# The opening of a fused transformer kernel put in another order: x and queries loaded first, the mask behind them; keys, values and score maxima dealt out in single blocks

## The chip, the cores and the metric

The kernel runs on one core of a Trainium2 chip. The metric is device time in microseconds (us) of one execution; the median of three runs is what is compared. The engines are TensorE (PE in the profile; its weight loads are PEld), VectorE (DVE), ScalarE (ACT), GpSimd (POOL) and SyncE (SP), which here only issues transfers.

## What is computed

Two layers on a batch of 2 with 256 rows of 256 channels, and a context of 4096 rows. Only the first attention matters for this change:

```python
h = layernorm(x)                                   # (2, 256, 256)
q = h @ Wq.T + bq ; k = ctx @ Wk.T + bk ; v = ctx @ Wv.T + bv      # 16 heads of 16
energy = where(mask == 0, -1e9, q @ k.T / sqrt(16))                # (2, 16, 256, 4096)
x = x + (softmax(energy) @ v) @ Wo.T + bo
```

Behind it come a gated convolution block, a quantised feed-forward block, a second cross-attention with an additive mask, a self-attention with rotary positions and a routed feed-forward block. They are the same in both kernels.

## The kernel before, in words

Every engine has its own program, written out by hand in `build`; the order in each is that of the code, and semaphores tie them together. All tiles lie in one SBUF tensor, `arena`, and one PSUM tensor, `psum`, so the trace names only these two; line numbers tell the steps apart.

**Keys, values, units.** The context of batch 0 is taken in 8 chunks of 512 rows. `project_keys(0, c, f)` (L1728) multiplies chunk `c` with half `f` of the key weights: one 128x512 block in float32, which the trace shows as 4 matmul records. `project_values(0, c, i)` (L1738) makes half a chunk of values, 8 records of 128x256. Both write into a ring of three PSUM banks (4 to 6), which ScalarE empties: `copy_keys` (L725, L726: a bf16 copy and a float32 copy) and `copy_values` (L731). Scores must be as exact as float32, so each key piece is split into three bf16 parts: VectorE takes the rest and casts it (`split_keys`, L1084, L1086), GpSimd makes the third part (`low_part`, L647), SyncE stores the parts in DRAM (`store_k`, L461) and loads them again stacked by head, 6 rows of parts to each channel (`load_stack`, L469: 6 transfers for a quarter of the context, two chunks). Queries take the same way (`split_queries`, L1069 to L1076; `store_queries`, L489; `load_queries`, L497). The pieces go through three float32 buffers `K32` and six places `KPT`, in the order of `piece_number`.

**Maxima.** Softmax needs each row's maximum. A *unit* is `scores(n)` (L1756): two 96x512 matmuls in bf16 into one of two pairs of PSUM banks; `row_tops(n)` (L1100) on VectorE reduces the 128x1024 result to a column of maxima. Unit n waits for the maximum of unit n - 2 (semaphore `s_maxed`). There are 32 units for the first head group; units 0 to 7 need quarter 0 of the stack, 8 to 15 quarter 1, and so on. Only when all 32 are done can `turn_max` (L1770) and the first turned scores (L1785) run, from which on exponentials (L748) and weighted values (L1803) take their turn.

**The opening.** PE first does key blocks, the transposes of the normalised x (`turn_x`, L1861) and the query projections (`project_queries_of`, L1869), with key blocks between. VectorE turns the mask into bf16 in 8 parts (`mask_part`, L1093), PE sums them (L1895), VectorE reads the sum (L1192, L1194) and writes a flag: PE branches on it (L2114) into a version without mask matmuls, `attend(False)`. The inputs have no masked place, so this version runs.

**Rounds.** In `attend` rounds `c` from 4 to 10 follow. In each half of a round PE does one key block (while c < 8), one value block of four matmuls, and then the 2 or 3 units that `UNITS_AT` gives it, in one run. VectorE does the split of the key piece and then the maxima.

**Loads.** SyncE issues the key weights, the columns of biases, x, the query and value weights, and chunks 3 to 5; ScalarE issues chunks 0 to 2 and the mask (4 transfers of 1 MB) at once. There are six slots for chunks; 6 and 7 follow when the values of chunks 0 and 1 are copied.

## Time and profile before

| | us |
|---|---|
| median of 3 runs (lowest to highest) | 1007.73 (1007.71 to 1008.43) |
| the profiled execution's own time | 1003.05 |
| its span in the trace | 1001.0 |
| PE busy | 905.0 (90%) |
| VectorE busy | 604.5 (60%) |
| ScalarE busy | 479.5 (48%) |
| first turned scores start (L1785) | 120.03 |

The span runs from the first to the last instruction of the profiled execution; the execution's own time is 2.05 us longer. All times of instructions below are counted from the span's start. A row of the timeline gives start, duration, engine, line and tiles, how many instructions it merges, and in brackets how long the engine had been idle and what ended that. PEclk is the granted TensorE clock, 1.00 being 2.4 GHz and 0.50 being 1.2 GHz.

### The profile page before, as it was taken

The page shows a single profiled execution, that of the slowest core. Times are in us where ns is not written, and L with a number is a line of the kernel's source. Part 1 is how long each engine was busy: PE and PEld are TensorE (multiplying, and loading weights), DVE is VectorE, ACT ScalarE, POOL GpSimd, SP SyncE. Part 2 cuts the span into 40 slices and gives each one's busy share as a digit, 9 for nine tenths or more (in the row PEclk, how much of TensorE's full clock was granted, in tenths as well). Part 3 has the DMA queues.
Part 4 walks back from the last instruction along what each step waited for, and adds up shares of the span by engine and source line. Part 5 has one row for each costly group of instructions (what it writes and reads, how often), then busy time and mean ns, then how long its engine had stood idle before and what let it go on. Part 6 is the DMA issues. An engine that isn't in the chain of part 4 may idle for free.

```text
span 1001.0 us, 15431 instructions
## 1 busy us (share of the span) xinstructions
PE 905.0 (90%) x6066; PEld 540.6 (54%) x6068; DVE 604.5 (60%) x1075; ACT 479.5 (48%) x951; POOL 105.7 (11%) x118
## 2 busy tenths in 40 slices
PE   6786799999999999999998899588999989988788
PEld 3444444444555555455544677354875854555656
DVE  3876577787885447888843586858414127188240
ACT  2232366777775557777788532225213110676111
POOL 1421011111000000000000200101000007155000
PEclk9999899999999999999999999779999989999889
DMA  9772823445323112222522700705438350000000
GB/s 358 218 202 93 259 79 107 133 127 163 101 66 105 33 32 65 64 67 74 191 96 76 261 1 1 253 25 184 163 133 303 118 168 1 1 1 2 0 1 22
DMA packets 68837, 108.70 MB, mean 109 GB/s; under 512 B 7062, under 2 KB 42902, under 8 KB 66838
## 3 DMA queue, kind: packets, MB, share of 16 engines
q1 hardware_dynamic: 67372, 101.92, 32.0%
q10 hardware_dynamic: 1392, 5.77, 1.4%
...
## 4 chain that ended last, share of the span: by engine, by line
PE 79%; DVE 8%; ACT 7%; issue 3%; DMA 2%; SPq 0%; POOL 0%; ACTq 0%; DVEq 0%
PE psum L1803 13%; PE psum L1785 11%; PE psum L1756 10%; PE psum L2172 6%; PE psum L2145 5%; PE psum L1934 5%; PE psum L1738 5%; PE psum L1728 4%; PE psum L2265 4%; PE psum L1947 3%; ACT arena L748 3%; DVE arena L1100 2%; PE psum L2313 2%; PE psum L2401 1%; PE psum L2298 1%
## 5 line engine op out<-in xcount | busy, mean ns | idle before, releaser
L1100 DVE TENSOR_REDUCE arena<-psum 128x1 f32<-128x1024 f32 x256 | 300.5, 1218 | 111.6 <-PE psum L1756 111.5
L748 ACT ACTIVATE arena<-psum 128x512 f32<-128x512 f32 x512 | 264.7, 604 | 63.4 <-PE psum L1785 62.3
L1785 PE MATMUL psum<-arena 99*128 99x256 bf16 x1024 | 161.0, 275 | 10.4 <-ACT arena L748 4.8
L1756 PE MATMUL psum<-arena 96*128 96x512 bf16 x512 | 152.2, 383 | 18.1 <-DVE arena L1100 11.4
L1785 PEld LDWEIGHTS psum<-arena 99*128 99x128 bf16 x1024 | 80.0, 97 | 109.2 <-ACT arena L748 50.6
L1803 PE MATMUL psum<-arena 128*32 128x256 f32 x2048 | 136.8, 385 | 0.0
L1803 PEld LDWEIGHTS psum<-arena 128*32 128x32 f32 x2048 | 53.5, 109 | 75.5 <-ACT arena L748 36.9
L1728 PE MATMUL psum<-arena 128*128 128x512 f32 x128 | 64.2, 630 | 5.6 <-DMA arena<-ctxT 5.6
L1756 PEld LDWEIGHTS psum<-arena 96*128 96x128 bf16 x512 | 49.3, 99 | 35.7 <-DVE arena L1100 18.8
L1738 PE MATMUL psum<-arena 128*128 128x256 f32 x256 | 64.2, 395 | 1.0 <-ACT arena L726 1.0
L647 POOL TENSOR_TENSOR arena<-arena 128x512 bf16<-128x512 f32 x34 | 41.5, 1221 | 210.0 <-DVE arena L1086 202.3
L2172 PE MATMUL psum<-arena 128*128 128x256 f32 x256 | 59.9, 389 | 0.0
L1738 PEld LDWEIGHTS psum<-arena 128*128 128x128 f32 x256 | 48.6, 196 | 19.6 <-issue 13.4
L2145 PE MATMUL psum<-arena 128*128 128x512 f32 x128 | 56.1, 593 | 0.0
L725 ACT ACTIVATE arena<-psum,arena 128x512 bf16<-128x512 f32 x32 | 22.0, 687 | 66.5 <-PE psum L1728 49.8
L731 ACT ACTIVATE arena<-psum 128x512 f32<-128x512 f32 x32 | 19.1, 597 | 71.1 <-PE psum L1738 71.1
L2172 PEld LDWEIGHTS psum<-arena 128*128 128x128 f32 x256 | 49.1, 196 | 6.5
L1934 PE MATMUL psum<-arena 128*128 128x256 f32 x192 | 47.0, 404 | 3.5 <-ACT arena L812 0.9
L1934 PEld LDWEIGHTS psum<-arena 128*128 128x128 f32 x192 | 38.2, 202 | 11.1 <-ACT arena L920 1.3
L2265 PE MATMUL psum<-arena 128*128 128x512 f32 x96 | 43.2, 611 | 0.7 <-ACT arena L810 0.7
L1728 PEld LDWEIGHTS psum<-arena 128*128 128x128 f32 x128 | 24.5, 200 | 29.3 <-issue 22.1
L1947 PE MATMUL psum<-arena 128*128 128x256 f32 (+1 forms) x160 | 36.4, 388 | 4.2 <-ACT arena L908 2.2
...
## 6 DMA issues: line engine op xcount, KB each, us to landing
...
kparts<-arena SPq DMA_DIRECT2D x32, 384.0 KB, 3.3
...
arena<-mask ACTq DMA_DIRECT2D x4, 1024.0 KB, 13.4
...
```

The costliest lines, as they stand in the source:

```text
L748: nc.scalar.activation(PR[step % 4][:, pair * CH:(pair + 1) * CH], ring_bank(slot), ACT.Exp)\
L1100: nc.vector.tensor_reduce(MX[g % 2][:, col:col + 1], unit_banks(n).rearrange("p b n -> p (b n)"), AX.X, ALU.max).then_inc(s_maxed, 1)
L1728: last = nc.tensor.matmul(ring_bank(slot), WK[:, k, f * P:(f + 1) * P], CTX[n % SLOTS][:, k, :], start=(k == 0), stop=(k == CT - 1))
L1738: last = nc.tensor.matmul(ring_bank(slot)[:, v * 256:(v + 1) * 256], CTX[n % SLOTS][:, k, (2 * i + v) * P:(2 * i + v + 1) * P], WV[:, k, : ...
L1756: last = nc.tensor.matmul(out, q, KST[g % 2][0:ROWS, j, at], start=True, stop=not masked, skip_group_check=True)
L1785: last = nc.tensor.matmul(ring_heads(slot)[:, u, :], KST[gg % 2][0:KROWS, j, kc * P:(kc + 1) * P], QST[0:KROWS, G * g + j, b * S:(b + 1) * S],
L1803: last = nc.tensor.matmul(PV[32 * j:32 * (j + 1), :], V_flat[:, at:at + 32], PR[step % 4][:, j * S:(j + 1) * S], start=(kc == 0), stop=(kc ...
L1934: last = nc.tensor.matmul(out, weights[:, k, m * P:m * P + width], xs[k], start=(k == 0), stop=(k == n - 1))
L1947: last = nc.tensor.matmul(out, lhs[k], weights[:, k, :], start=(k == 0 and not biased), stop=(k == n - 1), skip_group_check=biased)
L2145: last = nc.tensor.matmul(psum[:, unit % 3, :], QC[:, c, w * P:(w + 1) * P], CTXT[w // 2][:, c, n * 512:(n + 1) * 512], start=(c == 0), st ...
L2172: last = nc.tensor.matmul(psum[:, 6, 0:256], PT1[:, k * P:(k + 1) * P], CTXK[w // 2][:, k, :], start=(k == 0), stop=(k == KC - 1), skip_gr ...
L2265: last = nc.tensor.matmul(psum[:, bank, :], HTF[:, c, i * P:(i + 1) * P], WQKV[which][:, c, half * HALF:(half + 1) * HALF], start=(c == 0) ...
```

## The change

All of it lies in the first 120 us.

1. **Loads.** SyncE issues x and the query weights right behind the key weights, then the columns, chunks 2 and 3 and the value weights. ScalarE issues chunks 0 and 1, loads its table, waits until x has landed, and only then issues the mask. Chunks 4 and 5 are issued later, behind quarter 0 of the stack.
2. **PE's opening.** The transposes of x come after two key blocks instead of three; both query projections come before the keys of chunk 2. The last value block of chunk 0 moves from before the branch to behind it.
3. **VectorE and GpSimd.** The scaled queries of batch 1 go to a buffer of their own, `QREST`, and are split only after the keys of chunk 3; the flag is read before the pieces of chunk 2 (second half) and 3 are split. ScalarE takes the square root before the first key copies.
4. **Rounds.** Rounds 4 to 12 instead of 4 to 10. Keys still end with round 7, but only 12 units run by then instead of 22, and values stand still in rounds 5 and 7; the value block is done in two pieces (`project_value`), with a unit before each and behind the last. VectorE does the first maximum of a half round before the split.
5. **SyncE's order.** The queries of batch 1 are stored before the keys of chunk 4 and loaded behind chunk 7; the three small loads that waited for the mask move there too.

```diff
 RAMP = 5
-VALUES_AT = {3: 0, 4: 1, 5: 2, 6: 3, 7: 4, 8: 5, 9: 6, 10: 7}
-ROUNDS = 11
-UNITS_AT = {4: (2, 2), 5: (3, 3), 6: (3, 3), 7: (3, 3), 8: (2, 2), 9: (3, 3)}
+VALUES_AT = {3: 0, 4: 1, 6: 2, 8: 3, 9: 4, 10: 5, 11: 6, 12: 7}
+ROUNDS = 13
+UNITS_AT = {4: (2, 2), 5: (1, 1), 6: (2, 2), 7: (1, 1), 8: (3, 2), 9: (3, 2), 10: (3, 2), 11: (3, 2)}
 
...
         HT = [f32(at, 512) for at in (44816, 24064)]
+        QREST = f32(53632, 512)
         WQ = f32(53120, 512).rearrange("p (c f) -> p c f", c=CT)
...
 
-            return 2 * NCH * b + 2 * c + f + (2 if b else min(c, 2))
+            return 2 * NCH * b + 2 * c + f + (2 if b else (c >= 1) + (c >= BRANCH))
 
         def query_piece(b):
-            return 2 + 3 * b
+            return 2 + 7 * b
 
...
             sp.dma_start(WK, t["wkT"].rearrange("(c p) f -> p c f", p=P)).then_inc(wk_loaded, 16)
-            sp.dma_start(COLT, t["cols"]).then_inc(cols_loaded, 16)
             sp.dma_start(X, t["x"].rearrange("(t p) c -> p t c", p=P)).then_inc(x_loaded, 16)
             sp.dma_start(WQ, t["wqT"].rearrange("(c p) f -> p c f", p=P)).then_inc(wq_loaded, 16)
+            sp.dma_start(COLT, t["cols"]).then_inc(cols_loaded, 16)
+            for c in range(2, 4):
+                sp.dma_start(CTX[c], ctx_chunk(0, c)).then_inc(ctx_loaded[c], 16)
             sp.dma_start(WV, t["wvT"].rearrange("(c p) f -> p c f", p=P)).then_inc(wv_loaded, 16)
-            for c in range(3, SLOTS):
-                sp.dma_start(CTX[c], ctx_chunk(0, c)).then_inc(ctx_loaded[c], 16)
             sp.dma_start(arena[ROWS:KROWS, 0:8192], t["ones"]).then_inc(q_stacked, 16)
...
             load_stack(0, 0)
-            store_queries(1)
+            for c in range(4, SLOTS):
+                load_ctx(0, c, 0)
             for c in range(2, NCH):
+                if c == BRANCH:
+                    store_queries(1)
                 for f in range(CT):
...
                 if c == 3:
-                    sp.wait_ge(mask_step, 8)
-                    sp.dma_start(arena[ROWS:KROWS, 8192:16384], t["ones"]).then_inc(late_loaded, 16)
-                    sp.dma_start(BV, t["rows"][:, ROW_AT["bv"]:ROW_AT["bv"] + 256].broadcast_to((P, 256)))\
-                      .then_inc(late_loaded, 16)
-                    sp.dma_start(AW, t["A"].rearrange("(t p) s -> p t s", p=P)).then_inc(on["bm_loaded"], 16)
                     chunks_stored(2)
...
                 if c == 4:
-                    load_queries(1)
-                if c == 5:
                     first_values_done(1)
                     load_ctx(0, 7, 0)
+                    load_queries(1)
+                    sp.dma_start(arena[ROWS:KROWS, 8192:16384], t["ones"]).then_inc(late_loaded, 16)
+                    sp.dma_start(BV, t["rows"][:, ROW_AT["bv"]:ROW_AT["bv"] + 256].broadcast_to((P, 256)))\
+                      .then_inc(late_loaded, 16)
+                    sp.dma_start(AW, t["A"].rearrange("(t p) s -> p t s", p=P)).then_inc(on["bm_loaded"], 16)
+                if c == 5:
                     chunks_stored(4)
...
 
-            def low_part(r):
-                rest, parts = K32[r % 3], KPT[place(r)]
+            def low_part(r, rest):
+                parts = KPT[place(r)]
                 nc.gpsimd.tensor_tensor(parts[:, 2, :], rest, parts[:, 1, :], ALU.subtract).then_inc(k_low, 1)
...
                 b, c, f = idx // (2 * NCH), idx // 2 % NCH, idx % 2
+                r = piece_number(b, c, f)
                 pool.wait_ge(k_split, 2 * (idx + 1))
-                low_part(piece_number(b, c, f))
-                if idx in (1, 3):
-                    pool.wait_ge(q_split, 5 * (c + 1))
-                    low_part(query_piece(c))
+                low_part(r, K32[r % 3])
+                if idx == 1:
+                    pool.wait_ge(q_split, 5)
+                    low_part(query_piece(0), K32[query_piece(0) % 3])
+                if idx == 2 * BRANCH - 1:
+                    pool.wait_ge(q_split, 10)
+                    low_part(query_piece(1), QREST)
 
...
             load_ctx(1)
-            load_ctx(2)
+            act.wait_ge(built, 3)
+            nc.scalar.activation(TABLES[:, 0:1], ONES[:, 0:1], ACT.Sqrt)
+            act.wait_ge(x_loaded, 16)
             for i in range(4):
                 load_mask(i)
-            act.wait_ge(built, 3)
-            nc.scalar.activation(TABLES[:, 0:1], ONES[:, 0:1], ACT.Sqrt)
 
...
             act.wait_ge(cols_loaded, 16)
-            copy_keys(0, 0, 0)
-            copy_keys(0, 0, 1)
             act.wait_ge(ln_var, 1)
             nc.scalar.activation(SD[:, 0:4], SD[:, 4:8], ACT.Sqrt).then_inc(ln_sd, 1)
-            for c in range(1, ROUNDS):
+            for c in range(ROUNDS):
                 for i in range(2):
...
 
-            def split_queries(b):
-                n, r = 5 * b, query_piece(b)
-                rest, parts = K32[r % 3], KPT[place(r)]
-                if r >= 3:
-                    dve.wait_ge(k_low, r - 2)
+            def scale_queries(b, rest):
                 dve.wait_ge(first_psum, b + 1)
...
                                             DH ** -0.5, ALU.add, ALU.mult).then_inc(q_split, 1)
+
+            def split_queries(b, rest, n):
+                r = query_piece(b)
+                parts = KPT[place(r)]
+                if turn_at(r) > 1:
+                    dve.wait_ge(k_stored[place(r)], stores_ahead(r))
+                dve.wait_ge(q_split, n)
+                nc.vector.tensor_copy(parts[:, 0, :], rest).then_inc(q_split, 1)
+                dve.wait_ge(q_split, n + 1)
+                nc.vector.tensor_tensor(rest, rest, parts[:, 0, :], ALU.subtract).then_inc(q_split, 1)
                 dve.wait_ge(q_split, n + 2)
-                nc.vector.tensor_copy(parts[:, 0, :], rest).then_inc(q_split, 1)
-                dve.wait_ge(q_split, n + 3)
-                nc.vector.tensor_tensor(rest, rest, parts[:, 0, :], ALU.subtract).then_inc(q_split, 1)
-                dve.wait_ge(q_split, n + 4)
                 nc.vector.tensor_copy(parts[:, 1, :], rest).then_inc(q_split, 1)
...
             split_keys(0, 0, 1)
-            split_queries(0)
+            scale_queries(0, K32[query_piece(0) % 3])
+            split_queries(0, K32[query_piece(0) % 3], 2)
             copy_turned_x(1)
...
                 mask_part(i)
-            split_queries(1)
-            split_keys(0, 2, 0)
-            split_keys(0, 2, 1)
+            scale_queries(1, QREST)
             for i in range(4, 8):
                 mask_part(i)
-            split_keys(0, 3, 0)
+            split_keys(0, 2, 0)
             dve.wait_ge(first_psum, 3)
...
             nc.vector.tensor_scalar(FLAG, FLAGF[0:1, 0:1], 0.0, None, ALU.is_lt).then_inc(mask_step, 1)
+            split_keys(0, 2, 1)
+            split_keys(0, 3, 0)
             split_keys(0, 3, 1)
+            split_queries(1, QREST, 7)
             for c in range(BRANCH, ROUNDS):
                 for i in range(2):
-                    if c < NCH:
-                        split_keys(0, c, i)
-                    for _ in range(UNITS_AT.get(c, (0, 0))[i]):
-                        row_tops(n)
-                        if n == UNITS - 1:
-                            split_max(0)
-                        n += 1
+                    for turn in range(max(UNITS_AT.get(c, (0, 0))[i], 1)):
+                        if turn < UNITS_AT.get(c, (0, 0))[i]:
+                            row_tops(n)
+                            n += 1
+                        if turn == 0 and c < NCH:
+                            split_keys(0, c, i)
+            split_max(0)
             for step in range(GROUPS * KC):
...
 
+            def project_value(b, c, i, v):
+                slot, n = VALUE_AT[b, c, i], load_number(b, c, b)
+                if v == 0:
+                    pe.wait_ge(ctx_loaded[n % SLOTS], 16 * (n // SLOTS + 1))
+                    ring_free(slot)
+                for k in range(CT):
+                    last = nc.tensor.matmul(ring_bank(slot)[:, v * 256:(v + 1) * 256],
+                                            CTX[n % SLOTS][:, k, (2 * i + v) * P:(2 * i + v + 1) * P],
+                                            WV[:, k, :], start=(k == 0), stop=(k == CT - 1))
+                if v == 1:
+                    last.then_inc(ring_filled, 1)
+
             def project_values(b, c, i):
-                slot, n = VALUE_AT[b, c, i], load_number(b, c, b)
-                pe.wait_ge(ctx_loaded[n % SLOTS], 16 * (n // SLOTS + 1))
-                ring_free(slot)
                 for v in range(2):
-                    for k in range(CT):
-                        last = nc.tensor.matmul(ring_bank(slot)[:, v * 256:(v + 1) * 256],
-                                                CTX[n % SLOTS][:, k, (2 * i + v) * P:(2 * i + v + 1) * P],
-                                                WV[:, k, :], start=(k == 0), stop=(k == CT - 1))
-                last.then_inc(ring_filled, 1)
+                    project_value(b, c, i, v)
 
...
                 n = 0
+                project_values(0, 0, 1)
                 for c in range(BRANCH, ROUNDS):
                     for i in range(2):
+                        last = n + UNITS_AT.get(c, (0, 0))[i]
                         if c < NCH:
                             project_keys(0, c, i)
-                        if c in VALUES_AT:
-                            project_values(0, VALUES_AT[c], i)
-                        for _ in range(UNITS_AT.get(c, (0, 0))[i]):
+                        for v in range(2):
+                            if n < last:
+                                scores(n, masked)
+                                n += 1
+                            if c in VALUES_AT:
+                                project_value(0, VALUES_AT[c], i, v)
+                        if n < last:
                             scores(n, masked)
...
             project_keys(0, 0, 1)
-            project_keys(0, 1, 0)
             pe.wait_ge(built, 6)
...
             turn_x(1)
-            project_keys(0, 1, 1)
+            project_keys(0, 1, 0)
             pe.wait_ge(wq_loaded, 16)
             project_queries_of(0)
+            project_keys(0, 1, 1)
+            project_queries_of(1)
             project_keys(0, 2, 0)
             project_keys(0, 2, 1)
-            project_queries_of(1)
             project_keys(0, 3, 0)
...
             last.then_inc(first_psum, 1)
-            project_values(0, 0, 1)
             pe.wait_ge(mask_step, 10)
...
```

On PE, in the opening up to the branch (L1728 keys, L1861 transposes, L1869 queries, L1738 values, L1895 mask sums), there stood (float32 matmuls count once here and leave two records in the trace):

```order
L1728 MATMUL psum<-arena 128x512 x6
L1861 MATMUL psum<-arena 128x128 x8
L1728 MATMUL psum<-arena 128x512 x2
L1869 MATMUL psum<-arena 128x256 x4
L1728 MATMUL psum<-arena 128x512 x4
L1869 MATMUL psum<-arena 128x256 x4
L1728 MATMUL psum<-arena 128x512 x2
L1738 MATMUL psum<-arena 128x256 x4
L1728 MATMUL psum<-arena 128x512 x2
L1895 MATMUL psum<-arena 2x512 x16
L1738 MATMUL psum<-arena 128x256 x4
```

and now, where the same steps have lines L1737, L1881, L1889, L1747 and L1915:

```order
L1737 MATMUL psum<-arena 128x512 x4
L1881 MATMUL psum<-arena 128x128 x8
L1737 MATMUL psum<-arena 128x512 x2
L1889 MATMUL psum<-arena 128x256 x4
L1737 MATMUL psum<-arena 128x512 x2
L1889 MATMUL psum<-arena 128x256 x4
L1737 MATMUL psum<-arena 128x512 x6
L1747 MATMUL psum<-arena 128x256 x4
L1737 MATMUL psum<-arena 128x512 x2
L1915 MATMUL psum<-arena 2x512 x16
```

The transposes and both query projections moved ahead by one key block and more, and a value block left the place before the branch.

On PE, in the first rounds (keys, values, and units at L1756), there stood, for the second half of round 4 and the first of round 5:

```order
L1728 MATMUL psum<-arena 128x512 x2
L1738 MATMUL psum<-arena 128x256 x4
L1756 MATMUL psum<-arena 128x512 x4
L1728 MATMUL psum<-arena 128x512 x2
L1738 MATMUL psum<-arena 128x256 x4
L1756 MATMUL psum<-arena 128x512 x6
```

and now (units at L1770), for the last values of chunk 0, round 4, and the first key block of round 5:

```order
L1747 MATMUL psum<-arena 128x256 x4
L1737 MATMUL psum<-arena 128x512 x2
L1770 MATMUL psum<-arena 128x512 x2
L1747 MATMUL psum<-arena 128x256 x2
L1770 MATMUL psum<-arena 128x512 x2
L1747 MATMUL psum<-arena 128x256 x2
L1737 MATMUL psum<-arena 128x512 x2
L1770 MATMUL psum<-arena 128x512 x2
L1747 MATMUL psum<-arena 128x256 x2
L1770 MATMUL psum<-arena 128x512 x2
L1747 MATMUL psum<-arena 128x256 x2
L1737 MATMUL psum<-arena 128x512 x2
```

A unit now stands between a key block and half a value block, where two or three stood in a run.

On SyncE, from the stores of chunk 1's keys on (L461 stores of keys, L489 of queries, L497 loads of queries, L469 loads of the stack, L474 loads of chunks), there stood:

```order
L461 DMA kparts<-arena 128x3x512 x2
L497 DMA arena<-qparts 16x16x256 x6
L469 DMA arena<-kparts 16x4x1024 x6
L489 DMA qparts<-arena 128x2x256 x3
L461 DMA kparts<-arena 128x3x512 x4
L514 DMA arena<-ones 3x8192
L515 DMA arena<-rows 128x256
L517 DMA arena<-A 128x4x16
L469 DMA arena<-kparts 16x4x1024 x6
L474 DMA arena<-ctxT 128x2x512
```

and now (lines L462, L490, L498, L470, L475):

```order
L462 DMA kparts<-arena 128x3x512 x2
L498 DMA arena<-qparts 16x16x256 x6
L470 DMA arena<-kparts 16x4x1024 x6
L475 DMA arena<-ctxT 128x2x512 x2
L462 DMA kparts<-arena 128x3x512 x4
L470 DMA arena<-kparts 16x4x1024 x6
L475 DMA arena<-ctxT 128x2x512
L490 DMA qparts<-arena 128x2x256 x3
L462 DMA kparts<-arena 128x3x512 x2
L475 DMA arena<-ctxT 128x2x512
```

Two chunk loads stand behind quarter 0 of the stack, and the stores and loads of the second queries moved behind quarter 1 and chunk 6.

## Rows read from the trace of the kernel before

**Rows 1.** Waits between 46 and 120 us: waiter, releaser, us, times, longest.
```profile
PE psum L1756 <- DVE arena L1100: 8.7, 8, 1.2
```
**Rows 2.** Timeline of PE and DVE in the rounds and at their end.
```profile
59.40 3.48 DVE L1100 TENSOR_REDUCE arena<-psum 128x1 f32<-128x1024 f32 x3
...
60.67 0.61 PE L1756 MATMUL psum<-arena 96*128 96x512 bf16 x2 [1.16 <-DVE arena L1100]
61.11 1.88 PE L1728 MATMUL psum<-arena 128*128 128x512 f32 x4
62.83 1.89 PE L1738 MATMUL psum<-arena 128*128 128x256 f32 x8
...
101.73 1.87 PE L1756 MATMUL psum<-arena 96*128 96x512 bf16 x4 [5.78 <-DMA arena<-kparts]
...
103.40 3.45 PE L1738 MATMUL psum<-arena 128*128 128x256 f32 x8
...
116.67 0.61 PE L1770 MATMUL psum<-arena 128*3 128x128 bf16 x8
...
120.03 0.91 PE L1785 MATMUL psum<-arena 99*128 99x256 bf16 x4 [2.75 <-ACT arena L739]
```
**Rows 3.** Stretches: bounds, length, busy us (instructions) by engine, PEclk, DMA share, GB/s.
```profile
2.00:4.00 2.00, 0.00 (x0) 0.00 (x0) 0.00 (x0) 0.00 (x0) 0.98 (x3) 1.00 0.79 256
4.00:6.00 2.00, 0.40 (x1) 0.43 (x2) 0.00 (x0) 1.16 (x1) 0.00 (x0) 1.00 1.07 392
6.00:8.00 2.00, 2.00 (x3) 0.74 (x3) 0.00 (x0) 0.33 (x2) 0.00 (x0) 1.00 1.06 373
...
18.00:20.00 2.00, 2.00 (x3) 0.70 (x3) 1.93 (x5) 0.00 (x0) 0.79 (x1) 0.50 0.97 391
...
60.00:70.00 10.00, 8.18 (x30) 4.81 (x31) 7.38 (x8) 2.76 (x5) 1.86 (x2) 1.00 0.96 275
```
**Rows 4.** Timeline of the opening: PE, ACT, its queue, and DVE.
```profile
2.29 2.52 ACTq L707 DMA_DIRECT2D arena<-mask  x4
...
5.60 8.05 PE L1728 MATMUL psum<-arena 128*128 128x512 f32 x12 [5.60 <-DMA arena<-ctxT]
...
11.97 0.69 ACT L725 ACTIVATE arena<-psum,arena 128x512 bf16<-128x512 f32 x1 [1.25 <-PE psum L1728]
...
13.41 1.41 DVE L1043 BATCH_NORM_STATS2 arena<-arena 128x6 f32<-128x256 f32 x4 [13.41 <-DMA arena<-x]
...
16.48 1.42 PE L1861 MATMUL psum<-arena 128*128 128x128 f32 x8 [2.83 <-DVE arena L1054]
...
21.10 1.95 PE L1869 MATMUL psum<-arena 128*128 128x256 f32 x8
...
26.32 1.94 PE L1869 MATMUL psum<-arena 128*128 128x256 f32 x8
...
44.12 2.46 PE L1738 MATMUL psum<-arena 128*128 128x256 f32 x8
...
44.94 0.14 DVE L1194 TENSOR_SCALAR arena<-arena 1x1 int32<-1x1 f32 x1
...
46.42 1.88 PE L1728 MATMUL psum<-arena 128*128 128x512 f32 x4
```
**Rows 5.** The page: a group of instructions (third parts), and the stores of pieces.
```profile
L647 POOL TENSOR_TENSOR arena<-arena 128x512 bf16<-128x512 f32 x34 | 41.5, 1221 | 210.0 <-DVE arena L1086 202.3
...
kparts<-arena SPq DMA_DIRECT2D x32, 384.0 KB, 3.3
```
**Rows 6.** Timeline of SP's issues: second column is the time that issuing takes.
```profile
26.88 1.41 SPq L489 DMA_DIRECT2D qparts<-arena  x3
...
35.94 3.75 SPq L469 DMA_DIRECT2D arena<-kparts  x6
...
50.45 5.76 SPq L469 DMA_DIRECT2D arena<-kparts  x6
```
**Rows 7.** Loads of a context chunk issued between 55.5 and 57 us.
```profile
DMA to landing us min/median/max: 5.4/5.4/5.4
```

## The prediction

> **What bounds the kernel now.** Everything the change touches lies ahead of the first turned scores, at 120.03 us of a span of 1001.0 [rows 2]; the 881.0 us behind it keep their instructions. So I read the opening only: first the waits, then the timeline of PE and VectorE, then the stretches with their granted clock, then SyncE's issues. The reader is to see that neither PE nor VectorE is full there, though PE is busy 90% of the whole span. From the first key block of round 4 (46.42) [rows 4] to `turn_max` (116.67) [rows 2] PE takes 70.3 us. Its work there, at full clock: a key block starts 1.72 us before what follows it (61.11 to 62.83), a value block lasts as long (1.89 against 1.88), so 1.73, and a single unit takes 0.44 (60.67 to 61.11) [rows 2]. Eight key blocks are 13.8, fourteen value blocks 24.2, 32 units 14.1: 52.1 us. The other 18.2 us are waits. 8.7 of them are units that wait for the maximum two before, eight waits of 1.2 us at most [rows 1]: three units stand in a run, PE could do one in 0.44 us, but VectorE needs 3.48 / 3 = 1.16 us for each [rows 2]. 5.8 us are unit 24 waiting for quarter 3 of the stack, since chunk 7's keys come so late [rows 2]. After that stall four unit matmuls take 1.87 us, a value block 3.45 [rows 2], against 0.9 and 1.89: some 2.5 us lost to a slow clock. About 1.2 us are small change.
>
> Ahead of 46.42 the chain is x (landed at 13.41, seen by VectorE), its transposes (16.48), queries, mask sums, flag [rows 4].
>
> **x.** Ahead of x or beside it now go the key weights (0.26 MB), x itself (0.52) and chunks 0 and 1 (1.05): 1.83 MB. By 6 us the transfers had moved 2 x 256 + 2 x 392 GB/s = 1.30 MB, and then 373 GB/s [rows 3]: the rest takes 1.4 us, so x lands at **7.4**. The bounds are 5.6, when chunk 0 was there, and 13.4 as before [rows 4]. From x to the transposes it took 16.48 - 13.41 = 3.1 us [rows 4]: 10.5. A wait is added: the mask's four issues stand between x and ScalarE's square root, 2.52 us of issuing [rows 4], where the statistics alone need about 2. That is half a microsecond, 11.0, and it is free: PE still has the second key block, which ScalarE found ready at 11.97 [rows 4], so the transposes start at 11.8. Behind ScalarE's wait are also the first key copies; they come after the root, at about 10.2 instead of 9.5, and VectorE takes them only after the transposed x. The mask itself, 4.2 MB, starts at 8 instead of 3 us, behind less other traffic; VectorE asks for its first part at about 23, so its move costs nothing. If it came later than 25, each microsecond would count.
>
> **Opening on PE.** Transposes 1.3 (16.48 to the next key block), to 13.1; keys of chunk 1, first half, to 14.8; queries 0. From queries 0 to queries 1 it was 26.32 - 21.10 = 5.2 us [rows 4], with VectorE's splits between, and it is the same steps now: queries 1 at 20.0, done at 21.8. Three key blocks (5.2), a value block (1.7) and a key block (1.7): 30.4. The 16 mask sums are eight times a unit's two matmuls, 3.5: 33.9, if VectorE has made all eight parts; it no longer has the second queries' split and three of the key splits in between. The flag was ready at 45.08, 0.96 after the sums ended at 44.12 [rows 4]: 34.9 now. The branch is not seen, because a value block covered it: at least nothing, at most 46.42 - 45.08 = 1.3 us [rows 4]. I take 1.3, since that cover has moved behind the branch: 36.2, value block to 37.9.
>
> **Chunk 4** now decides. SyncE stored queries 0 at 26.88, 5.8 after PE began them, and had issued quarter 0 at 39.69 [rows 6]: 12.8 later. Now 14.8 + 5.8 + 12.8 = 33.4, and the chunk lands 5.4 later [rows 7]: 38.8. So round 4 starts at **38.8 instead of 46.42: 7.6 us**. 37.9 is the lower bound; should the chunk be as slow as twice the 5.4, it is 44.
>
> **Rounds.** The work stays 52.1. What is late next:
> - Chunk 6, moved from a place that hid it. PE is through round 4 (8.7: four float blocks of 1.73 and four units) and round 5 (4.3) at 51.8. SyncE needs the third part of chunk 3's last piece. Three pieces are split only after the flag, on VectorE and GpSimd in turn, 1.22 us a step [rows 5], four steps: 39.8. Stored in 3.3 [rows 5], six issues in 3.75 to 5.76 [rows 6], 5.4 to land: 52.3 to 54.3. PE waits 0.5 to 2.5 us; I take 1.5.
> - VectorE. Rounds 8 to 11 hold 20 units (23.2 us at 1.16) against 20 x 0.44 + 8 x 1.73 = 22.6 us of PE: 0.6. The third unit of a half stands close behind, and handing over costs a little: between 0.6 and the old 8.7, I take 2.5, near the lower end, as half a value block (0.87) plus a unit (0.44) is 1.3 us, more than 1.16.
> - Quarter 3. Chunk 7's keys are done at 38.8 + 8.7 + 4.3 + 1.5 + 8.7 + 4.3 = 66.3; splits 4, store 3.3, issues 3.75 to 5.76, landing 3.3: 80.7 to 82.7. Unit 24 is due at 66.3 + 1.5 + 12 x 1.16 = 81.7. The 5.8 us go; one could come back. Taken as nothing.
> - Clock: one stall may still cost part of the 2.5 us: 1. Small change: 1.1.
>
> 52.1 + 1.5 + 2.5 + 1 + 1.1 = 58.2: `turn_max` at 97.0. From there to the turned scores 3.36 us, unchanged (120.03 - 116.67) [rows 2]: **100.4**, so 19.7 us saved. The moved small loads and the second queries' transfers are due only for the turned scores and for batch 1; they are issued by 60 us. The stack of the next group (24 transfers) starts about 16 us earlier too, so its lead stays.
>
> **Sum.** The profiled execution took 1003.05 us (span 1001.0 and 2.05 around it): 983.4. The median of the three runs is 4.7 above it, and I carry that over: 1007.7 - 19.7 = **988.0**. A measurement of this kernel can tell about 0.2%, 2 us, from no change.
>
> **A rule against the change.** The clock did fall when PE had been idle: after the gap before 16.48 it was 0.50, that is 1.2 GHz, in 18 to 20 us [rows 3, 4]. It stayed 1.00 from 60 to 70 us [rows 3], though PE stopped 1.16 us in every half round [rows 2]. The Trainium skill, "TensorE: Matmul & The Clock Gate", section "A second HAM failure mode: psum-queue depth-cycling", says that small idle gaps between groups of bf16 matmuls which go round the PSUM banks can be enough to make the clock swing. That is how the alternating units work. By that rule rival 3 would come true; the row of 60 to 70 us disagrees with it.
>
> **Rivals.**
> 1. *SyncE's queue becomes the bound* (0.13). Chunks 4 and 6 and quarter 3 each arrive 3 us later than worked out and each stall costs 2.5 us of clock: 16.5, less the 2.5 already in the sum: 14 lost, saved 5.7, 1002; with one or two of them, about 995. For it: all three stand in one queue with margins of a microsecond. Against it: stores landed in about 3.3, and the queue carries less of the mask.
> 2. *x is not earlier* (0.05): the transfers share the engines otherwise than assumed and x lands at 13.4. Transposes at 16.5, 4.7 later, all behind it too: saved 15.0, 992.7. That would be the change not doing what it says.
> 3. *PE falls to 1.2 GHz in the alternation* (0.05, **slower than before**). Every gap between single units counts as idling. All 52.1 us take 104.2; 38.8 + 104.2 + 1.5 + 1.1 + 3.4 = 149.0, 29 later than before: 1036.7. It decides from the point where 20.7 of the 52.1 us of work run at half speed. For it: the fall after 16.48. Against it: the clock in 60 to 70 us.
> 4. *The gain is given back behind 120 us* (0.03): groups 0 and 1 wait for chunks of batch 1 that come no earlier: about 1007.
>
> **How the numbers follow.** My forecast has 0.74: saved 14 to 24, 984 to 994. The lower end takes the branch at nothing, no wait for chunk 6, the clock kept and VectorE's 0.6: 19.7 + 0.9 + 1.5 + 1 + 1.9 = 25, not all together. Rivals 1 and 2 are faster as well: 0.92 together; within 0.2% 0.03 (rival 4), slower 0.05 (rival 3). The range 984 to 996 holds the forecast, rival 2 and half of rival 1.
>
> **What would show it.** Right: statistics of x at 7 to 8 us; transposes behind the second key block; round 4 at 38 to 40; the waits on the maximum down from 8.7 to 2 or 3; no wait of 5.8 at unit 24; `turn_max` near 97 and turned scores near 100. Wrong: PEclk under 0.9 between 40 and 95 us (rival 3); waits of PE on chunk loads over 3 us (rival 1); a stretch from the first turned scores to the end that is longer than 881 us (rival 4).

## The result, and the profile after

| us | before | after |
|---|---|---|
| median of 4 timed executions | 1008.08 (1007.71 to 1008.71) | 995.80 (995.08 to 996.69) |
| profiled execution's own time / span | 1003.05 / 1001.0 | 995.86 / 994.1 |
| round 4 starts | 46.42 | 43.20 |
| `turn_max` | 116.67 | 105.61 |
| first turned scores | 120.03 | 108.97 |
| from there to the end | 881.0 | 885.1 |

The ratio is 0.9895, interval 0.9864 to 0.9925: faster by 7.6 to 13.7 us (the two medians differ by 12.3). The median 995.80 lies 7.8 us above the forecast of 988.0, and within the range of 984 to 996 only because that was drawn wide enough for half of rival 1. (Runs that were disturbed are left out, among them one of before at 1558.6 us.) At the first turned scores, where all that the change touches is over, 11.1 us are gained of the 19.7 forecast.

The opening after, in the timelines of the engines (rows as in [rows 4]):

```profile
8.39 1.80 ACTq L714 DMA_DIRECT2D arena<-mask  x4
8.39 1.41 DVE L1048 BATCH_NORM_STATS2 arena<-arena 128x6 f32<-128x256 f32 x4 [8.39 <-DMA arena<-x]
...
11.61 1.34 PE L1881 MATMUL psum<-arena 128*128 128x128 f32 x8
...
19.62 1.99 PE L1889 MATMUL psum<-arena 128*128 128x256 f32 x8 [1.50 <-DVE arena L1064]
...
31.20 3.61 PE L1915 MATMUL psum<-arena 128*2 128x512 bf16 x16
...
35.56 0.14 DVE L1200 TENSOR_SCALAR arena<-arena 1x1 int32<-1x1 f32 x1
...
36.86 2.49 PE L1747 MATMUL psum<-arena 128*128 128x256 f32 x8 [2.05 <-issue]
...
43.20 3.78 PE L1737 MATMUL psum<-arena 128*128 128x512 f32 x4 [3.85 <-DMA arena<-ctxT]
```

Up to the branch this is the predicted chain, no step off by more than 1.0 us and the flag by 0.8. Then PE stands still for chunk 4, and its next key block lasts 3.78 us instead of 1.88.

What SyncE issues between 20 and 90 us in after (second column: the time that issuing takes):

```profile
20.23 1.98 SPq L490 DMA_DIRECT2D qparts<-arena  x3
...
29.93 3.93 SPq L498 DMA_DIRECT2D arena<-qparts  x6
34.05 3.75 SPq L470 DMA_DIRECT2D arena<-kparts  x6
37.84 1.11 SPq L475 DMA_DIRECT2D arena<-ctxT  x2
...
60.13 3.82 SPq L498 DMA_DIRECT2D arena<-qparts  x6
...
65.40 1.04 SPq L462 DMA_DIRECT2D kparts<-arena  x2
72.91 3.76 SPq L470 DMA_DIRECT2D arena<-kparts  x6
...
85.03 14.94 SPq L470 DMA_DIRECT2D arena<-kparts  x23
```

L470 is quarter 0 at 34.05, quarter 2 at 72.91 and quarter 3 at 85.03 (there merged with later loads); L462 at 65.40 stores chunk 5's keys.

And PE's timeline where the units need quarters 2 and 3:

```profile
79.02 0.59 PE L1770 MATMUL psum<-arena 96*128 96x512 bf16 x2 [0.93 <-DMA arena<-kparts]
...
91.54 1.02 PE L1770 MATMUL psum<-arena 96*128 96x512 bf16 x4 [2.65 <-DMA arena<-kparts]
92.40 1.54 PE L1747 MATMUL psum<-arena 128*128 128x256 f32 x4
```

Unit 24, which waited until 101.73 [rows 2], is released at 91.54: 10 us earlier, yet 9 to 11 later than the landing that I had worked out (80.7 to 82.7). The waits of PE from 34 to 115 us in after (waiter, releaser, us, times, longest):

```profile
PE psum L1737 <- DMA arena<-ctxT: 3.9, 1, 3.9
PE psum L1770 <- DMA arena<-kparts: 3.6, 2, 2.6
...
PE psum L1770 <- DVE arena L1107: 1.3, 2, 0.8
```

The 8.7 us behind VectorE [rows 1] are down to 1.3. Transfers took the place of both old waits: that is rival 1's mechanism. The granted clock, in stretches (columns as in [rows 3]):

```profile
40.00:44.00 4.00, 0.80 (x1) 0.50 (x2) 2.88 (x4) 0.00 (x0) 2.55 (x3) 0.50 0.90 268
44.00:48.00 4.00, 4.00 (x7) 1.65 (x6) 0.13 (x1) 0.98 (x2) 0.17 (x1) 0.50 1.00 350
...
54.00:64.00 10.00, 10.00 (x35) 5.38 (x34) 8.97 (x13) 4.99 (x8) 3.77 (x4) 1.00 0.97 292
...
90.00:97.00 7.00, 5.46 (x18) 3.56 (x19) 3.70 (x4) 0.56 (x1) 0.00 (x0) 0.76 0.63 214
```

1.2 GHz (0.50) stands beside the wait for chunk 4, and 0.76 behind the one for quarter 3; in between, where units alternate with blocks, PE is busy all of 10 us at 2.4 GHz.

### The profile page after: what moved, and what is told of

Read it like the earlier page. It is cut to its first block, busy times and chain, and to the rows that moved or that the text cites. A ratio compares the mean times of both kernels' runs of the same rounds, so it can differ in the third digit from the quotient of the medians.

```text
span 994.1 us, 15431 instructions
## 1 busy us (share of the span) xinstructions
PE 909.2 (91%) x6066; PEld 544.4 (55%) x6068; DVE 605.2 (61%) x1075; ACT 479.4 (48%) x951; POOL 105.4 (11%) x118
## 4 chain that ended last, share of the span: by engine, by line
PE 77%; DVE 7%; ACT 6%; DMA 5%; issue 3%; SPq 2%; POOL 1%; ACTq 0%; DVEq 0%
PE psum L1817 13%; PE psum L1799 11%; PE psum L1770 9%; PE psum L2191 6%; PE psum L2164 5%; PE psum L1953 5%; PE psum L2284 4%; PE psum L1747 4%; PE psum L1966 3%; DMA kparts<-arena 3%; PE psum L1737 3%; ACT arena L755 3%; PE psum L2332 2%; PE psum L2420 1%; PE psum L2317 1%
## 5 line engine op out<-in xcount | busy, mean ns | idle before, releaser
L1770 PE MATMUL psum<-arena 96*128 96x512 bf16 x512 | 153.9, 383 | 8.6 <-DVE arena L1107 4.0
L1737 PE MATMUL psum<-arena 128*128 128x512 f32 x128 | 64.4, 632 | 10.1 <-DMA arena<-ctxT 9.3
L1747 PE MATMUL psum<-arena 128*128 128x256 f32 x256 | 66.1, 396 | 2.0 <-issue 2.0
L1770 PEld LDWEIGHTS psum<-arena 96*128 96x128 bf16 x512 | 49.5, 99 | 28.3 <-DVE arena L1107 11.9
L2191 PE MATMUL psum<-arena 128*128 128x256 f32 x256 | 59.5, 387 | 0.0
L1747 PEld LDWEIGHTS psum<-arena 128*128 128x128 f32 x256 | 48.4, 194 | 18.4 <-issue 10.1
L1953 PE MATMUL psum<-arena 128*128 128x256 f32 x192 | 48.6, 413 | 3.4 <-ACT arena L817 0.9
L1953 PEld LDWEIGHTS psum<-arena 128*128 128x128 f32 x192 | 39.3, 208 | 11.5 <-ACT arena L925 1.3
L1737 PEld LDWEIGHTS psum<-arena 128*128 128x128 f32 x128 | 24.6, 201 | 34.1 <-issue 23.0
```

The source lines that it names most:

```text
L1737: last = nc.tensor.matmul(ring_bank(slot), WK[:, k, f * P:(f + 1) * P], CTX[n % SLOTS][:, k, :], start=(k == 0), stop=(k == CT - 1))
L1747: last = nc.tensor.matmul(ring_bank(slot)[:, v * 256:(v + 1) * 256], CTX[n % SLOTS][:, k, (2 * i + v) * P:(2 * i + v + 1) * P], WV[:, k, : ...
L1770: last = nc.tensor.matmul(out, q, KST[g % 2][0:ROWS, j, at], start=True, stop=not masked, skip_group_check=True)
L1953: last = nc.tensor.matmul(out, weights[:, k, m * P:m * P + width], xs[k], start=(k == 0), stop=(k == n - 1))
L2191: last = nc.tensor.matmul(psum[:, 6, 0:256], PT1[:, k * P:(k + 1) * P], CTXK[w // 2][:, k, :], start=(k == 0), stop=(k == KC - 1), skip_gr ...
```

## The experiments

**Theories.** A: the stalls that are left come from round trips through DRAM, slow while mask and chunks fill the transfer engines, and from what stands ahead in SyncE's queue. B: the gain is that of VectorE's waits and of x; what is missing was lost elsewhere. The yardstick is the first turned scores (short: FT), because single executions of the same kernel spread by several us behind it, as the first pair shows.

**before_again and after_again** repeat both kernels unchanged. In the diffs below "..." stands for lines left out.

> The kernel before, unchanged, profiled once more. The profiled execution of before took 1003.05 us, the timed ones 1007.7 to 1008.7; behind the first turned scores the changed kernel took 885.1 us where before took 881.0, with the same instructions. Theory (granted clock): the stretch behind the turned scores varies by 4 to 5 us with where the clock falls at the stage borders near 550 to 700 us; this profile then shows the turned scores at 120.0 again and either 881 us (time 1003) or 885 to 886 us (time 1008) behind them, with the difference in PEclk between 540 and 720 us. Rival (given back): the changed kernel really is slower behind the opening because its loads come in another order; then this profile shows 881 again and an own time near 1003.

> The changed kernel once more, since single executions of the kernel before spread from 1000.2 to 1009.6 us. Theory (the opening is reproducible, the stretch behind it is not): turned scores at 108.5 to 109.5 again, and behind them between 877 and 886 us with PEclk between 500 and 740 us deciding; median of the timed runs 990 to 997. Rival (the changed order makes the stretch behind longer for good): 885 us behind the turned scores again.

Before: FT at 121.46, 1004.63 us. After: FT at 110.01, median 994.07 of six; ratio 0.988 (0.9838 to 0.9922). FT thus repeats to about 1.4 us. Behind FT before took 881.0 again, and after 883.9 instead of 885.1; that is taken up at the end of the next section. Whole times spread more: 13 executions of before that stood beside the first of these runs lay between 1000.16 and 1009.62, with a median of 1003.91. The forecast's starting point 1007.7 was near one end of that, and the 2 us that it took for what a measurement can tell were too few for single executions.

**old_rounds** keeps after's opening and takes back the three tables and both loops of the rounds.

```diff
-VALUES_AT = {3: 0, 4: 1, 6: 2, 8: 3, 9: 4, 10: 5, 11: 6, 12: 7}
-ROUNDS = 13
-UNITS_AT = {4: (2, 2), 5: (1, 1), 6: (2, 2), 7: (1, 1), 8: (3, 2), 9: (3, 2), 10: (3, 2), 11: (3, 2)}
+VALUES_AT = {3: 0, 4: 1, 5: 2, 6: 3, 7: 4, 8: 5, 9: 6, 10: 7}
+ROUNDS = 11
+UNITS_AT = {4: (2, 2), 5: (3, 3), 6: (3, 3), 7: (3, 3), 8: (2, 2), 9: (3, 3)}
```

> The changed kernel with the tables and the loops of the rounds of before (two or three units in a run, keys until round 7 with 22 units between): only the opening is changed. Theory (most of the gain is in the rounds): from round 4 at 43.2 on it takes the old 70 us plus 2.7 for the slow clock: turned scores at 115 to 119, time 1002 to 1007. Rival (the gain is the opening): turned scores below 112, time below 999.

FT 120.20, later than either side expected; median 1004.43; ratio 0.9996 (0.997 to 1.0023). PE's timeline shows why:

```profile
43.86 3.78 PE L1737 MATMUL psum<-arena 128*128 128x512 f32 x4 [4.98 <-DMA arena<-ctxT]
47.43 2.50 PE L1747 MATMUL psum<-arena 128*128 128x256 f32 x8
49.77 1.03 PE L1770 MATMUL psum<-arena 96*128 96x512 bf16 x4
...
101.93 1.87 PE L1770 MATMUL psum<-arena 96*128 96x512 bf16 x4 [6.06 <-DMA arena<-kparts]
```

and in before the first units stand at

```profile
49.86 1.03 PE L1756 MATMUL psum<-arena 96*128 96x512 bf16 x4
```

Round 4 starts 2.6 us earlier than in before, not 7.6, because chunk 4 is late; and its first key and value block, at a low clock behind that wait, take 5.9 us instead of 3.4. At the first units all is lost (49.77 against 49.86). From there the two kernels keep the same pace to unit 24, at 101.93 and 101.73. The chain that ended last (`--critical`) runs through key blocks, ScalarE's copies, VectorE's splits and maxima, and only then through chunk 7's store and quarter 3:

```profile
89.83 1.16 POOL arena L650
...
91.01 3.98 DMA kparts<-arena
```

The last store goes out as soon as GpSimd has made its third part. So SyncE's queue holds nothing up here: quarter 3 comes when PE and VectorE have come to chunk 7. The new opening by itself gives nothing, since chunk 4 and the clock take back what it gains.

**new_rounds_alone** is the other half: before's opening and queues, with the new tables and loops (the diff above turned round, and `project_value`).

> The kernel before with the new tables and loops of the rounds alone (keys of batch 0 early, units between half value blocks); opening, SyncE's order and loads as before. Theory (the rounds bring nearly all, since quarter 3's landing decides and the keys end 16 us earlier): from round 4 at 46.4 to 47.9 on, turned scores at 109 to 113, time 993 to 998. Rival (both parts are needed, as the new opening's x and queries give 5 us when the rounds are new): turned scores at 114 to 117, time 998 to 1003.

FT 107.95, median 993.76; ratio 0.9912 (0.9886 to 0.9939). Round 4 starts at 46.47, 3.3 us later than in after, and yet FT comes 1.0 us earlier (about what FT repeats to, so: no later), and earlier than either side expected. From round 4's start to `turn_max` it takes 58.1 us, not 62.4. PE waits for no quarter of the stack (waits from 35 to 120 us; the third behind VectorE, 0.45 us at 117.07, lies behind FT, so 1.3 us count):

```profile
PE psum L1728 <- DMA arena<-ctxT: 1.8, 1, 1.8
PE psum L1761 <- DVE arena L1100: 1.7, 3, 0.8
```

So the rounds alone, tables and single blocks together, carry the whole measured gain: with keys done by the middle of the stretch, quarter 3's stores and loads lie beside units, and SyncE still has before's order, in which the second queries are loaded earlier (57.09 to 62.17, not 60.13 to 63.95) and the three small loads stand ahead of them, at 47.88. Which share belongs to the tables and which to the single blocks this run does not tell; before's opening with the new tables in runs was not tried. The length is also my 58.2 for the rounds, where nothing but chunk 6 is late.

**new_tables_in_runs** is after with its new tables, but units in one run behind the value block and the split ahead of the maxima, as before.

```diff
-                        for v in range(2):
-                            if n < last:
-                                scores(n, masked)
-                                n += 1
-                            if c in VALUES_AT:
-                                project_value(0, VALUES_AT[c], i, v)
-                        if n < last:
+                        if c in VALUES_AT:
+                            project_values(0, VALUES_AT[c], i)
+                        for _ in range(UNITS_AT.get(c, (0, 0))[i]):
```

> The changed kernel with its new tables (keys end earlier, 13 rounds), but the units of a half round in one run behind the value block, and VectorE splits first, as before. Theory (alternation ends the waits on the maximum): waits of units on VectorE come back, 1.2 us in each of the halves with 3 units and little in those with 2: turned scores 3 to 6 us later than 109.0, time 999 to 1002. Rival (what counts is that the keys end early, so that quarter 3 is there): within 1.5 us of the changed kernel, 994.5 to 997.5.

FT 108.86 against 108.97, as the rival has it; median 993.86; ratio 0.9888 (0.9836 to 0.9939). Up to `turn_max` PE waits 3.5 us for maxima instead of 1.3, and 1.9 instead of 3.6 for the stack. While quarter 3 sets the end, the single blocks only move idle time from one wait to the next.

**chunks_early** issues chunks 4 and 5 with the first loads again.

```diff
+            for c in range(4, SLOTS):
+                sp.dma_start(CTX[c], ctx_chunk(0, c)).then_inc(ctx_loaded[c], 16)
...
-            for c in range(4, SLOTS):
-                load_ctx(0, c, 0)
```

> The changed kernel, but chunks 4 and 5 are issued in the first list of loads as before. Theory (place in SyncE's queue): chunk 4 is late only because it stands behind quarter 0 of the stack; round 4 then starts at 38 to 39.5 instead of 43.2, PE does not fall to half clock there, first turned scores at 101 to 104 instead of 109.0, time 988 to 991. Rival (the DMA engines are full until 28 us): 1 MB more ahead delays the mask and the first stores by 2.5 us, so key copies, mask sums and flag come later and quarter 0 lands later; turned scores at 106 to 109, time 993 to 996.

FT 107.96, median 994.12; ratio 0.99 (0.9848 to 0.9951). The wait for chunk 4 goes, but round 4 starts at 41.92, not at 38 to 39.5. With two more chunks on the transfer engines the stores of chunk 0's keys land later (the second in 13.1 us instead of 11.5), ScalarE's copies wait for free pieces, and the last key block before the mask sums for ScalarE: at 31.56 after 2.46 us instead of at 29.31. The branch's value block starts at 39.11, not 36.86, and of the 3.9 us about 1 is left, with quarter 3 at 90.53 after 2.59.

**mask_at_once** issues the mask at once, without the wait for x.

```diff
-            act.wait_ge(built, 3)
-            nc.scalar.activation(TABLES[:, 0:1], ONES[:, 0:1], ACT.Sqrt)
-            act.wait_ge(x_loaded, 16)
             for i in range(4):
                 load_mask(i)
+            act.wait_ge(built, 3)
+            nc.scalar.activation(TABLES[:, 0:1], ONES[:, 0:1], ACT.Sqrt)
```

> The changed kernel, but ScalarE issues the mask right behind chunks 0 and 1, without waiting for x. Theory (the chain to quarter 3 decides, not x): x lands at 11 to 13 instead of 8.4 and the transposes begin at 15 to 16.5, but the mask and with it the first stores land earlier; round 4 within 1.5 us of 43.2, turned scores within 2 us of 109.0. Rival (x first is worth what the opening gained): flag and round 4 later by 4 us and turned scores at 112 to 114, time 3 to 5 us more.

Rows of all engines in its opening:

```profile
9.86 1.40 DVE L1047 BATCH_NORM_STATS2 arena<-arena 128x6 f32<-128x256 f32 x4 [9.86 <-DMA arena<-x]
...
17.98 0.21 ACT L772 ACTIVATE arena<-arena 128x4 f32<-128x4 f32 x1 [12.03 <-DMA arena<-cols]
...
19.00 1.99 PE L1880 MATMUL psum<-arena 128*128 128x128 f32 x8 [7.49 <-DVE arena L1058]
```

x was only 1.5 us later (9.86 against 8.39). But the columns, which the change put behind the query weights in SyncE's queue, landed just before 17.98, ScalarE's root waited for them, and the transposes for the root. FT 114.33, 5.4 later than after, where the theory had expected at most 2 us; median 997.74; ratio 0.9948 (0.9926 to 0.997). The mask's wait is worth 5.4 us within this order, and it protects the columns more than x.

**half_mask** loads only the mask's first 128 rows and uses them for both halves (the second half of the mask is not read, 2.1 MB less).

```diff
-            for i in range(4):
+            for i in range(2):
                 load_mask(i)
...
-                if half == 0:
-                    dve.wait_ge(mask_loaded[qt], 32)
+                if i == 0:
+                    dve.wait_ge(mask_loaded[0], 32)
...
-                nc.vector.tensor_scalar(MASKB[:, qt, at], MASKI[:, qt, at], 0.0, MASKED, ALU.is_equal, ALU.mult)\
+                nc.vector.tensor_scalar(MASKB[:, qt, at], MASKI[:, 0, at], 0.0, MASKED, ALU.is_equal, ALU.mult)\
```

> The changed kernel, but the second 128 rows of the mask are not loaded: VectorE makes the second four parts from the first half's integers, so 2.1 MB less is moved in the opening and the masked places of those rows are not looked at. Theory (the DMA engines are full until 28 us and the stores of the first pieces wait in line): the first store lands before 24 instead of 27.8, queries 0 before 26 instead of 29.9, quarter 0 is issued at 28 to 31 instead of 34.1, chunk 4 lands at 37 to 40 instead of 43.2 and round 4 starts there at full clock; turned scores at 104 to 107. Rival (a store's landing takes 7 to 12 us for another reason, such as the many small rows in DRAM): landings and round 4 within 1 us of the changed kernel.

FT 105.06, median 989.05; ratio 0.9849 (0.9812 to 0.9885). The first store of keys, issued at 15.8 in both (columns: transfer, KB, median us from issue to landing), in after:

```profile
kparts<-arena SPq DMA_DIRECT2D x1, 384.0 KB, 12.0
```

and in half_mask:

```profile
kparts<-arena SPq DMA_DIRECT2D x1, 384.0 KB, 6.9
```

The queue then does all that follows earlier; half_mask's issues:

```profile
20.25 1.71 SPq L490 DMA_DIRECT2D qparts<-arena  x3
...
25.17 3.95 SPq L498 DMA_DIRECT2D arena<-qparts  x6
29.30 3.75 SPq L470 DMA_DIRECT2D arena<-kparts  x6
33.09 1.10 SPq L475 DMA_DIRECT2D arena<-ctxT  x2
```

The stores of queries 0 go out at the same time as in after (20.25 against 20.23) and land in 3.0 to 3.8 us instead of 7.5 to 8.8, so that their loads follow at 25.17, not 29.93. Chunk 4 is issued 4.75 us earlier and PE no longer waits for it. Round 4 starts at 38.63; that this is my forecast's 38.8 is partly chance, since PE's own work, at a low clock, sets it there and not the chunk. The load from the mask is what made the store round trip long.

**sp_order** moves SyncE's loads of the second queries and the three small loads from behind chunk 7 to behind quarter 3.

```diff
                 if c == 4:
                     first_values_done(1)
                     load_ctx(0, 7, 0)
-                    load_queries(1)
-                    sp.dma_start(arena[ROWS:KROWS, 8192:16384], t["ones"]).then_inc(late_loaded, 16)
...
             load_stack(0, 3)
+            load_queries(1)
+            sp.dma_start(arena[ROWS:KROWS, 8192:16384], t["ones"]).then_inc(late_loaded, 16)
...
```

> The changed kernel, but loading the queries of batch 1 and the three small loads stand behind quarter 3 of the stack in SyncE's queue instead of before the stores of chunk 5. Nothing else moves. Theory (SyncE's queue order sets when quarter 3 lands): quarter 2 is issued at 66 to 69 instead of 72.9, quarter 3 at 79 to 81 instead of 85.0, unit 24 does not wait or waits under 1 us at 84 to 87 instead of 91.5, turned scores at 103 to 105.5, 4 to 6 us of time. Rival (VectorE's splits of chunk 7's keys or the landing of stores sets it, whatever the queue holds): quarter 3 within 1.5 us of 85.0 and turned scores above 107.5.

FT 103.63, 5.3 us earlier than after; median 989.86; ratio 0.9864 (0.9818 to 0.9911). Its issues:

```profile
59.39 2.60 SPq L462 DMA_DIRECT2D kparts<-arena  x2
65.50 3.75 SPq L470 DMA_DIRECT2D arena<-kparts  x6
...
78.22 4.25 SPq L470 DMA_DIRECT2D arena<-kparts  x6
```

The stores of chunk 5's keys are issued at 59.39, not 65.40, quarter 2 at 65.50, not 72.91, quarter 3 at 78.22, not 85.03. No unit waits for the stack; chunk 4 still costs PE 4.34 us, and chunk 6 costs 0.77. The chain that ended last shows the change of bound. In after from 55 to 73 us it ran through the queue (start, us, what):

```profile
55.21 4.91 DMA qparts<-arena
...
65.95 6.88 DMA kparts<-arena
```

with the issues of the six and the three small loads between them. In sp_order, from 60 to 100 us, it has no transfer at all:

```profile
by line: PE psum L1747 47.0%; PE psum L1770 25.6%; PE psum L1737 10.7%; DVE arena L1107 9.8%; DVE arena L1091 3.6%; DVE arena L1093 2.1%; issue 1.8%
```

**all_three** joins sp_order, chunks_early and one more move: chunk 6's load ahead of quarter 1 of the stack.

> The changed kernel with chunks 4 and 5 in the first list of loads, chunk 6 issued ahead of quarter 1, and the queries of batch 1 and the small loads behind quarter 3. Theory (queue order, three places of it): no wait on a chunk above 1 us, round 4 at about 41.4 as in the run with chunks 4 and 5 early, chunk 6 at 54 instead of 57.9, unit 24 without a wait, turned scores at 98 to 101, time 7 to 10 us under the changed kernel. Rival (what one order gives the next stall takes): turned scores not below 103.

FT 102.53, between what theory and rival had, and 1.1 below sp_order, which is less than FT repeats to; median 987.30; ratio 0.9823 (0.9772 to 0.9873). PE waits for no transfer from 35 to 120 us, but the key block ahead of the mask sums waits 3.36 us for ScalarE, as in chunks_early, and the clock falls there (0.50 from 34 to 38 us): its branch block starts at 42.80, 5.9 later than in after.

**all_three_in_runs** is all_three with the units in runs.

> The kernel with all three changes of SyncE's order (turned scores at 102.5), with the units of a half round again in one run behind the value block. Theory (alternation pays once no stack load stalls PE): waits of units on VectorE of 3 to 6 us in all come back and stay, turned scores at 105 to 108. Rival (VectorE's total sets the pace either way): within 1 us of 102.5.

FT 106.42, 3.9 later than all_three, though its branch block starts 2.1 earlier (40.71); median 992.35; ratio 0.9887 (0.9858 to 0.9916). From that block to `turn_max` it takes 62.4 us against 56.4. PE in its rounds, from 73 us:

```profile
73.63 0.61 PE L1770 MATMUL psum<-arena 96*128 96x512 bf16 x2 [1.25 <-DVE arena L1107]
...
75.20 3.06 PE L1747 MATMUL psum<-arena 128*128 128x256 f32 x8
```

Up to `turn_max` waits for maxima are 4.4 us against 1.3, and the value block behind two of them lasts 3.06 instead of 1.89 us. Of the 6.0 us between the two stretches 1.7 are something else: here the low clock of the opening reached the first two blocks behind the branch, in all_three the mask sums ahead of it. That is also for the most part why the same opening ended 2.1 us apart in the two runs. Once no transfer sets the end, alternating is thus worth some 4 us; before that it is worth nothing.

**chunk4_early** is all_three with chunk 4 alone among the first loads and chunk 5 behind quarter 0 (these lines against after):

```diff
+            sp.dma_start(CTX[4], ctx_chunk(0, 4)).then_inc(ctx_loaded[4], 16)
...
-            for c in range(4, SLOTS):
-                load_ctx(0, c, 0)
+            load_ctx(0, 5, 0)
```

> As the kernel with all three changes of SyncE's order, but only chunk 4 is in the first list of loads and chunk 5 stays behind quarter 0. Theory (each 0.5 MB more in the opening delays mask and stores by 1.3 us): flag and round 4 1 to 1.5 us earlier than its 42.8 and 44.6, turned scores at 101 to 102, time 985 to 989. Rival (the opening's last wait is another): turned scores at 102.5 or later.

FT 98.86, median 984.04 (983.70 to 985.23); ratio 0.9816 (0.9791 to 0.9842). It is the fastest of all, and 2 us better than its theory. PE:

```profile
37.98 1.97 PE L1747 MATMUL psum<-arena 128*128 128x256 f32 x8 [2.05 <-issue]
39.78 1.88 PE L1737 MATMUL psum<-arena 128*128 128x512 f32 x4
42.85 0.59 PE L1770 MATMUL psum<-arena 96*128 96x512 bf16 x2 [1.19 <-DMA arena<-kparts]
```

Round 4 at 39.78, no stall over 1.2 us in the rounds, the granted clock 1.00 in each stretch of 10 us from 34 to 94, and 55.7 us to `turn_max`: 52.1 of work, 1.3 for maxima, 1.2 for quarter 0, 1.1 of the rest.

## Why the prediction was right and wrong

**x, transposes, queries, flag: right.** x landed at 8.4 (7.4), transposes 11.6 (11.8), queries 14.5 and 19.6 (14.8, 20.0), sums ended at 34.8 (33.9), flag ready 35.7 (34.9). The branch, which no row of before showed alone, was 2.05 us from the end of the sums to the value block, of which 35.70 to 36.86, 1.16, lie behind the flag: my upper bound of 1.3 was the right choice. What I did not see is that the root also waits for the columns, which stand behind the query weights now; mask_at_once shows that this makes the mask's wait a condition of the gain.

**Chunk 4: wrong, by the store's landing.** The step that failed is "12.8 later ... 33.4": I took the time from queries 0's store to the end of quarter 0's issue from before, as a fixed time. It took 17.6 us (20.23 to 37.80). The 4.8 us lie in one place. In before, SyncE issued the loads of queries 0 4.9 us behind their first store (26.88 [rows 6] to 31.80), whose parts had landed in 2.2 to 3.7 us:

```profile
31.80 3.96 SPq L497 DMA_DIRECT2D arena<-qparts  x6
```

In after this took 9.7 us (20.23 to 29.93), with landings of 7.5 to 8.8; from the loads to the end of quarter 0's issue it is 7.9 us in both. In before mask and chunks were through just ahead of these stores: the transfer engines carried 372 GB/s from 24 to 26 us and 130 from 26 to 28. Now the mask starts at 8.4 and its last part lands at 28.0, and the engines carry 383 to 418 GB/s from 16 to 28 us. The stores of chunk 0's keys took 12.0 and 11.5 us, chunk 1's 7.0 to 8.1. Chunk 4 was issued at 37.84 instead of 33.4: 4.4 late, and round 4 started 4.4 late. I had written of the mask that "its move costs nothing" and asked only when VectorE needs it; what it takes from other transfers I left out. half_mask shows that this is the cause: the same stores and loads of queries 0 lie 4.9 us apart again (20.25 to 25.17), and chunk 4 is issued 4.75 earlier. The sign was there in before: 3.3 us for a store [rows 5] is the median of 32, but the first two, at 20.8 and 22.3 beside 379 to 387 GB/s, took 8.7 and 8.1.

**Clock: mis-sized.** I allowed 1 us. Beside the 3.85 us gap, three steps of 1.73, 0.44 and 0.87 us at full speed took 3.57, 0.85 and 1.26 (43.20 to 48.88): 2.6 lost. Behind unit 24's wait, from 92.40 to 96.24, two pairs of half a value block and a unit took 3.84 instead of 2.61: 1.2 lost. Together 3.8. The length of the gap alone does not tell what a stall costs: behind 1.80 us in new_rounds_alone the next key block took 2.96 us (PEclk 0.62 from 61.3 to 65 us), behind 2.05 at the branch of chunk4_early none was slower and PEclk stayed 1.00.

**Quarter 3 "taken as nothing": wrong, by SyncE's queue.** Due at 80.7 to 82.7 by my sum, it landed at 91.4. Some 5 us of that came with PE: chunk 7's keys were done at 71.3, not 66.3. The rest arose behind them, since my sum had these keys split and stored at once. The queue is in order: it had to wait for the store of the second queries to land (60.1), issue their six loads and three small ones (to 65.4), and only then store chunk 5's keys, whose landing (6.88 us) held quarter 2 and with it the stores of chunks 6 and 7 (76.71); the last of them landed in 6.2 us where I had 3.3. I had called these loads "due only for the turned scores" and checked who needs them, not who stands behind them. sp_order takes just this out: quarter 3 is issued 6.8 us earlier, and FT gains 5.3.

**VectorE 2.5: too much.** Up to `turn_max` PE waited 1.3 us for maxima in after, in new_rounds_alone and in chunk4_early. **Chunk 6, 1.5 us:** no wait in after. Its load landed at about 58.4 instead of 52.3 to 54.3, but PE, 4.4 us late by chunk 4 and 2.6 by the clock, came to it only at 58.8. Elsewhere it cost 0.8 (sp_order), 1.8 (new_rounds_alone) and 2.2 (chunks_early).

**The rounds' sum.** Predicted 58.2, measured 62.4 = 52.1 of work + 3.6 for quarters 2 and 3 + 1.3 for maxima + 3.8 of clock + 1.6 that I did not take apart. With 4.4 at the start this makes the 8.6 us by which the first turned scores came later than 100.4. It is rival 1 with two of its three stalls. I had given it 0.13, and 995 for such a case; the time was 995.8. It should have been the forecast or near it: its reason against, "stores landed in about 3.3", was read from a stretch with other traffic.

**Rival 2** fell (x at 8.4). **Rival 3** fell: PEclk is 1.00 from 54 to 90 us of after, in the very rounds that alternate. The rule of the Trainium skill ("TensorE: Matmul & The Clock Gate", "A second HAM failure mode: psum-queue depth-cycling") does not come true here: by it, small idle gaps between such groups would have made the clock swing; with gaps of up to 0.8 us between units PE kept 2.4 GHz, and the low stretch of the first rounds stands behind the gap of 3.85 us.

**Where the gain was credited: wrong.** I had put 7.6 us to x and the opening, 6.2 to the maxima, 5.8 to quarter 3. Such savings do not add up while one chain ends last. By old_rounds and new_rounds_alone the opening gives 0 by itself, the rounds 12.1 of the 11.1 measured. In after the single blocks give 0 (new_tables_in_runs); with the transfers out of the way they give some 4 (all_three_in_runs), and so they may have a share in the 12.1, where PE waited for no quarter either. The opening pays once SyncE's order and chunk 4's place are mended as well: chunk4_early stands at 98.86 against 107.95 in new_rounds_alone, and 6.7 of these 9.1 us are round 4's earlier start (39.78 against 46.47).

**Behind the first turned scores.** 885.1 us in after, 883.9 in its repeat, but 881.0 in before, 881.0 in its repeat and 880.9 in old_rounds, with the same instructions. This looks like rival 4, and the repeat of before came out as the rival in its own expectation had it. But over the runs with the new rounds the stretch is anything from 877.5 (chunks_early) to 888.2 (all_three). Two stretches that begin 440 us behind the first turned scores, of after:

```profile
548.97:568.97 20.00, 17.58 (x88) 13.37 (x89) 12.98 (x40) 8.16 (x15) 0.81 (x3) 0.80 0.55 210
```

and of before:

```profile
560.03:580.03 20.00, 18.15 (x108) 14.44 (x108) 17.26 (x52) 9.78 (x20) 0.88 (x3) 1.00 0.57 212
```

After is granted 0.80 there and gets through 88 matmuls, before 1.00 and 108. The difference begins only at about 540 us of before, long after the first attention's start. What makes the clock fall in one execution and not in another was not tried and stays open; that it is a cost of this change is not shown, nor is it ruled out. The spread of before's whole time (999.8 to 1009.6) is as large.
